# Sharing out the blocks of two accumulators in the first of five sweeps over a graph's matrix

## What is computed

```
# layer 0
h = tanh(concat([x, t]) @ W1 + b1);  XB = x @ B.T
x = layernorm(x + h @ W2 + b2 + adj @ XB - rowsum(adj) * XB)
# layer 1 (Chebyshev terms, K = 3): three more products with adj
T1 = adj @ x;  T2 = 2 * (adj @ T1) - x;  T3 = 2 * (adj @ T2) - T1
x = layernorm(x + x @ w[0] + T1 @ w[1] + T2 @ w[2] + T3 @ w[3] + bias)
# layer 2
h_neigh = (adj @ x + x) / max(rowsum(adj) + 1, 1)
x = layernorm(x + l2norm(relu(concat([x, h_neigh]) @ W + b)))
# layer 3: the last 100 non-zeros of each row, weighted by powers of 1/2
out = w(adj) @ (x @ weight) + bias;  x = layernorm(x + out)
```

## Time and profile before

| | |
|---|---|
| median of 3 runs | 3067.41 us (3066.72 to 3070.59) |
| the profiled execution | 3066.3 us |
| its span, first to last instruction | 3064.5 us |
| busy share, PE / DVE / ACT | 96% / 92% / 77% |
| DMA | 1148.18 MB, mean 375 GB/s, 9 tenths busy in nearly every slice |
| granted TensorE clock | 9 tenths or more in all 40 slices |
| chain that ended last | PE 67%, DVE 23%, DMA 4%, ACT 3% |

### The profile page before, as it was taken

One profiled execution on the slowest core, in us unless ns is written; L12 is line 12 of the kernel. 1 busy time (PEld: TensorE's weight loads), 2 busy tenths in 40 slices (PEclk: granted clock), 3 DMA queues, 4 the chain that ended last, 5 costly groups with the idle time before them and its releaser, 6 DMA issues.

```text
span 3064.5 us, 35311 instructions
## 1 busy us (share of the span) xinstructions
PE 2933.3 (96%) x13488; PEld 2156.4 (70%) x13488; DVE 2816.1 (92%) x2385; ACT 2356.8 (77%) x1631; POOL 13.2 (0%) x31
## 2 busy tenths in 40 slices
PE   7999999999999998999989999998989999999998
PEld 5677778777788886888867888776766555555554
DVE  7998988898998889988899988999999899999997
ACT  5887877777877678777777776877777788888887
POOL 0000000000000000000000000000000000000000
PEclk9999999999999999999999999999999999999999
DMA  9999999999999999999999999989999999999996
GB/s 345 391 389 353 385 358 355 363 391 375 366 397 382 377 377 391 391 384 378 378 374 370 381 377 376 374 344 350 402 404 409 359 387 384 380 387 384 380 384 252
DMA packets 158935, 1148.18 MB, mean 375 GB/s; under 512 B 18016, under 2 KB 18256, under 8 KB 19504
## 3 DMA queue, kind: packets, MB, share of 16 engines
q1 hardware_dynamic: 157312, 1143.02, 95.1%
q0 software_dynamic: 1088, 2.48, 0.2%
q10 hardware_dynamic: 368, 0.43, 0.0%
HBM read 1143.75 MB, written 2.10 MB: 374 GB/s over the span
## 4 chain that ended last, share of the span: by engine, by line
PE 67%; DVE 23%; DMA 4%; ACT 3%; issue 2%; SPq 0%; ACTq 0%; DVEq 0%
PE ACC L934 26%; DVE lo L660 18%; PE ACC L941 15%; PE ACC L1063 14%; DMA raw<-in_at 4%; PE PSF L1077 4%; PE PST L1077 4%; ACT hi L466 2%; PE PST L957 1%; DVE SV L770 1%; PE PSF L1043 1%; PE PSF L1018 1%; PE PSF L1021 0%; DVE SV L777 0%; PE PSF L1016 0%
## 5 line engine op out<-in xcount | busy, mean ns | idle before, releaser
L660 DVE TENSOR_TENSOR lo<-raw,hi 128x2048 fp32r<-128x2048 f32 x832 | 1877.9, 2287 | 151.6 <-ACT hi L466 146.7
L466 ACT CAST hi<-raw 128x2048 fp32r<-128x2048 f32 x832 | 1584.0, 1912 | 519.9 <-PE ACC L934 323.7
L934 PE MATMUL ACC<-hi,T 128*128 128x512 f32 x4992 | 1281.4, 393 | 6.1 <-DVE T L618 4.3
L934 PEld LDWEIGHTS ACC<-hi,T 128*128 128x128 f32 x4992 | 935.7, 189 | 208.1 <-DVE T L618 4.6
L941 PE MATMUL ACC<-lo,T 128*128 128x512 f32 x3200 | 888.7, 400 | 95.1 <-DVE lo L660 87.8
L941 PEld LDWEIGHTS ACC<-lo,T 128*128 128x128 f32 x3200 | 589.3, 189 | 294.1 <-DVE lo L660 179.5
L675 DVE SCALAR_TENSOR_TENSOR M<-raw,M 128x512 bf16<-128x512 f32 x1008 | 636.6, 686 | 41.3 <-PE ACC L1063 24.7
L472 ACT ACTIVATE Wf<-ACC,w_bias 128x1024 fp32r<-128x1024 f32 x512 | 568.1, 1114 | 128.6 <-PE ACC L1063 128.0
L1063 PE MATMUL ACC<-M,rank_b 128*128 128x512 bf16 x2032 | 528.4, 382 | 8.2 <-ACT Wf L472 6.7
L1063 PEld LDWEIGHTS ACC<-M,rank_b 128*128 128x128 bf16 x2032 | 158.8, 98 | 266.5 <-issue 131.6
L1077 PE MATMUL PST<-Wf,S 128*128 128x512 f32 x512 | 209.2, 489 | 0.0
(11 more groups left out here) (165 smaller groups left out, 983.2 us busy)
## 6 DMA issues: line engine op xcount, KB each, us to landing
raw<-in_at SPq DMA_DIRECT2D x1088, 1024.0 KB, 6.7
SV<-in_x_cols SPq DMA_DIRECT2D x8, 256.0 KB, 12.3
out<-O POOLq DMA_DIRECT2D x7, 256.0 KB, 6.6
out<-O ACTq DMA_DIRECT2D x1, 256.0 KB, 2.0
w_sb<-in_w POOLq DMA_DIRECT2D x3, 64.0 KB, 9.1
bias<-in_bias_rows ACTq DMA_DIRECT2D x1, 128.0 KB, 9.4
l1w_sb<-in_l_w POOLq DMA_DIRECT2D x2, 64.0 KB, 8.2
rank_f<-in_rank_mats POOLq DMA_DIRECT2D x1, 128.0 KB, 9.9
```

What stands on the lines that cost most here:

```text
L466: nc.scalar.copy(hi[:, c % NH], raw[:, c % NR]).then_inc(hi_done, 1)
L660: tt(lo[:, c % NR], raw[:, c % NR], hi[:, c % NH].bitcast(f32), ALU.subtract).then_inc(lo_done, 1)
L934: ins = mm(acc[:, part], w, hi[:, p.c % NH, s, part], start=p.opens and s == 0 and i == 0, stop=False)
```

## The change

The order of groups in sweep 1 is replaced from row 3 on by a written list of single blocks (four pairs each). A P block stands for the next block of that row's P group, an S block likewise. P and S blocks of a row now take turns, and S blocks of a row stand among P blocks of the next one. Both accumulators are then open at the same time. Rows 0 to 2, sweeps 2 to 5 and the last layer keep their order.

```diff
     if k == 1:
-        for r in range(NB):
-            single, older = ("S", r, blocks[r:]), ("P", r, blocks[:r])
-            out += [single] if r == 0 else [single, older] if r < 3 else [older, single]
+        for r in range(3):
+            out += [("S", r, blocks[r:])] + ([("P", r, blocks[:r])] if r else [])
+
+        order = ("P3 P3 S3 P3 S3 S3 P4 S3 S3 P4 P4 S4 P4 S4 P5 S4 P5 S4 P5 P5 S5 P5 S5 P6 P6 S5 "
+                 "P6 P6 P6 P6 S6 P7 P7 P7 S6 P7 P7 P7 P7 S7")
+        left = {f"P{r}": blocks[:r] for r in range(3, NB)} | {f"S{r}": blocks[r:] for r in range(3, NB)}
+        for name in order.split():
+            out.append((name[0], int(name[1:]), left[name][:1]))
+            left[name] = left[name][1:]
+        assert not any(left.values())
         return out
...
         for kind, r, blocks in sweep_groups(k, NB):
-            acc_of[k, kind, r] = turn % 2
-            turn += 1
+            whole = [J for other, row, piece in sweep_groups(k, NB) if (other, row) == (kind, r) for J in piece]
+            if (k, kind, r) not in acc_of:
+                acc_of[k, kind, r] = turn % 2
+                turn += 1
+                group_order.append((k, kind, r))
             for J in blocks:
                 for pr in range(NP):
                     pairs.append(Pair(len(pairs), k, r, kind, block_of(k, r, NB), J, pr,
-                                      J == blocks[0] and pr == 0, J == blocks[-1] and pr == NP - 1, pr == 0))
-            group_order.append((k, kind, r))
+                                      J == whole[0] and pr == 0, J == whole[-1] and pr == NP - 1, pr == 0))
             group_end[k, kind, r] = row_end[k, r] = pairs[-1].c
```

## The result

| | before | changed |
|---|---|---|
| median (6 runs each) | 3069.41 us | 3057.48 us |
| ratio, with 95% interval | | 0.9958 (0.9948 to 0.9968) |
| profiled execution | 3066.3 | 3057.9 |
| start to the end of row 2 | 288.2 | 286.6 |
| rows 3 to 7 of sweep 1 (from here on: the stretch) | 456.8 | 447.0 |

The prediction was 3054.4 us with a range of 3045 to 3066. As a ratio it was 3054.4 / 3067.4 = 0.9958; the two medians of six runs alone give 0.9961. The four parts of a profiled execution are cut at TensorE's signal after pairs 95, 255 and 831.

The account below looks back on a forecast made before the run. TensorE bounds double runs; in single runs it waits for VectorE, then the DMA queue, losing 25.0 us. Of this 7.9 + 0.6 + 2.0 + 1.5 = 12.0 stay, 13.0 are won: median 3054.4 us, range 3045 to 3066.

Parts of the forecast that it names:

- What bounds it: Rows 3 to 7: TensorE bounds double runs, but waits for VectorE, then the queue, in single runs; 25.0 us lost.
- (a): Single blocks right behind a P group's end (places 4, 13, 22, 30, 39), with ScalarE's copies: 7.9 us stay lost.
- (b): Single blocks alone between double blocks, without copies (places 2, 11, 15, 17, 20, 25, 34): 0.6 us stay lost.
- The rival in which each block pays 1.6 us: All fifteen single blocks: 23.7 of 25.0 us stay lost, 3066.1 us, no change; chance 0.21.
- (c): Single blocks that still touch (places 4 and 5; 7 and 8): 0.7 and 1.3, together 2.0 us stay lost.
- (d): Landings, places 4 to 8 and 11 to 17: TensorE asks faster than the queue's 2.48 us a pair; 1.5 us lost.
- the prediction's own sign that (d) is wrong: ScalarE idle ahead of its `hi` split until the landing, in many pairs of places 4 to 17; no size given.
- The sum: Rows 3 to 7: 12.0 of 25.0 us stay lost, 13.0 are won; profiled execution 3053.3 us, median 3054.4.
- No value and no accumulator waited for: P blocks needing a row's value start 12 pairs after its end, and groups open late enough: no new TensorE wait.
- rule of totals: Skill page: interleaving regimes with different most-contended engines may help; so read, the whole 25.0 us won, 3042.4 us.
- the rule on repeated bubbles: Skill page: a repeated gap can mean too few buffers; the three `hi` buffers stay three, so 0 won.

Follow-up runs that it names:

- small splits and transfers: Kernel before, the 60 single pairs of rows 3 to 7 transfer, split and subtract half their columns, all matmuls kept: stretch 436.3 us against 456.8.
- split copies: Changed kernel, ScalarE's second copy of a finished P group one pair later, from row 3 on: stretch 442.0 us, median 3055.39 us, ratio to before 0.9949.
- half transfers: Changed kernel, the 60 single pairs of rows 3 to 7 transfer half their data, `hi` and `lo` at full size: stretch 442.2 us against 447.0.

## Why the prediction was right, point by point

- **What bounds it.** Right. TensorE's own work was 431 us in all kernels (432 predicted), the loss was 25.9 (25.0 predicted), and with small splits and transfers it goes from the single runs.
- **(a) The five blocks behind a P group.** Predicted 2.3, 1.3, 2.0, 1.3 and 1.0, together 7.9; measured 1.3, 1.3, 1.9, 1.3 and 1.3, 7.1; the 2.3 for place 4 was 1.0 too high. That the pile of `tanh` and copies moves to row 5 was right (1.9 at place 22, 1.3 at place 13), and the split copies showed the cause.
- **(b) Blocks alone.** Right for six of the seven: places 2, 11, 15, 20, 25 and 34 cost 0.34 us together (0.6 predicted). The rival in which each block pays 1.6 us fell with them. The seventh, place 17, was to last 7.2 to 7.4 us and lasted 9.4; that belongs to the next point.
- **(c) and (d), touching blocks and landings.** These terms were mis-sized: 2.0 + 1.5 = 3.5 predicted, and places 5, 7, 8 and 17 cost 7.9, or 6.7 in the second profile of the same kernel. The step that failed stands in both. (c) let VectorE's 2.22 us set the pace of places 7 and 8, with 2.0 us given back in place 6; (d) said "The six slots of `raw` lend some two or three pairs, and the double blocks ahead fill them". The trace has landings 2.48 us apart from pair 118 (place 5) to pair 139 (place 10), but for the late one, and ScalarE's split starts within 0.1 us of its landing in every pair of places 7, 8 and 17, and in 24 of the 56 pairs of places 4 to 17. That was the prediction's own sign that (d) is wrong. At this pace a double block gives back 4 x (2.72 - 2.48) = 1.0 us and a single one uses up 2.7, so place 6 had not filled the slots again. With half transfers the four places cost 1.7: some 5 of the 6.7 us are landings' (places 18 and 26 rose by 1.7 there, so the stretch fell by less). The bound of 5.9 us for (d) was for places 11 to 17 alone, and its 2.27 us a pair should be 2.20, as four single and three double blocks stand there; most of what the landings cost fell in places 5 and 8.
- **The sum.** 9.8 us were won in the stretch (11.5 in the second profile) and not 13.0. The rest of the medians' 11.9 isn't the change's in any way that I could show: the profiled execution is 8.4 faster, from 1.6 at the start, 9.8, 0.6 in sweeps 2 to 5, and 3.6 lost in the last layer (below). The start, the same code in every kernel, took 286 to 292 us in the twelve profiles, so parts outside the stretch scatter by more than the 3.2 us that the sum was off. That the recorded ratio is 0.9958 to the last digit is luck; that the time is in the range isn't, as the stretch alone puts it there.
- **No value and no accumulator waited for**, as predicted: the double blocks that open a group or need a new value cost 0.4 us or less.
- **The two readings of the Trainium skill's page.** The Trainium skill's "Perfetto Trace Analysis" (section "Optimization Strategy") read as a rule of totals promised the whole 25.0; the run gave 9.8 of it. Read as the rule on repeated bubbles it promised nothing, and 9.8 us of such waits went with no buffer added. Neither gave the size: what did was how many pairs of lead a double block gives back.

## What to carry to other kernels

Where two kinds of work on one stream are bound by different engines, take turns in pieces that the lead of the buffers can cover, and work out the lead that each piece uses up and gives back, for every stage of the stream: here VectorE's balance was positive at four pairs each (2.0 us given back, 1.6 used up), the queue's was not (1.0 and 2.7). This rule is worked out from the paces; no run changed the number of buffers or the length of the pieces. Once such turns have made the common engine the bound, small piles on other engines (two copies in a row) begin to cost what a long wait hid before: parting them won 2.2 to 3.8 us in the new order and nothing in the old one, counted to one pair past the stretch. Count past the end of the stretch, too: 1.2 us of what seemed won there had moved to the next pair. And when the stretch that was changed wins less than execution times scatter, compare its length in the profiles and not only the medians.

## What the runs showed of the hardware that I had not expected

**After nearly the same pause of TensorE the clock fell in one kernel and not in the other.** The last layer has the same instructions in every kernel, yet it took 728.9 us in both profiles of the changed kernel, 725.3 in the one before (725.2 to 725.7 in seven others), and 726.9 and 727.0 in two. Windows of the changed kernel (first TensorE's busy time, the clock is the third number from the end):

```profile
2352.80:2356.20 3.40, 1.40 (x7) 0.77 (x8) 3.30 (x7) 3.19 (x4) 0.00 (x0) 1.00 1.01 422
2356.20:2359.60 3.40, 3.40 (x10) 1.42 (x10) 3.33 (x7) 1.89 (x2) 0.00 (x0) 0.50 1.01 422
...
2369.70:2373.20 3.50, 1.40 (x7) 0.70 (x6) 2.90 (x7) 3.29 (x4) 0.00 (x0) 1.00 0.98 405
...
2980.80:2984.20 3.40, 1.30 (x6) 0.58 (x4) 2.16 (x4) 3.36 (x5) 0.00 (x0) 1.00 1.01 381
2984.20:2987.60 3.40, 3.36 (x8) 1.42 (x9) 1.46 (x3) 2.02 (x2) 0.00 (x0) 0.50 0.87 361
```

The first and the last of these places in the kernel before, 12.0 us later as its sweep 5 ends 12.0 us later:

```profile
2364.80:2368.20 3.40, 1.44 (x7) 0.81 (x8) 3.30 (x7) 3.19 (x4) 0.00 (x0) 1.00 1.01 419
2368.20:2371.60 3.40, 3.40 (x18) 1.75 (x16) 3.33 (x7) 2.93 (x3) 0.00 (x0) 1.00 1.01 422
...
2992.80:2996.20 3.40, 1.55 (x7) 0.82 (x8) 1.12 (x3) 3.19 (x4) 0.00 (x0) 1.00 1.01 390
2996.20:2999.60 3.40, 3.40 (x17) 1.83 (x16) 3.37 (x7) 2.85 (x3) 0.58 (x1) 1.00 0.58 207
```

At 0.50 of full speed, so at 1.2 GHz, TensorE did 10 and 8 matmuls where it did 18 and 17 at 2.4 GHz: some 1.7 us lost at each, and 3.6 in the whole layer. All of these falls stand right behind a pause of TensorE. Both kernels have one at a further place (at 2373 in the changed one, after the middle row, and at 2383 in the one before); at the other two places TensorE was busy for 1.40 and 1.30 us of the 3.4 ahead in the changed kernel and the clock fell, and for 1.44 and 1.55 in the one before and it did not. The two kernels with 726.9 and 727.0 us have two such falls, those near 725.3 have one. Why the same place falls in one kernel and not in another, no run here settles.

**A landing can be 2.1 us late in a full queue.** At 372 us one 16 KB packet of the instruction queue ran among those of pair 129's transfer, which landed 4.6 us after the one ahead of it where 2.5 is the rule. Such packets come every 1.5 to 38 us in this stretch of both traces. Whether one of them causes such a delay was not tried, but the twelve traces can be counted. They have 1253 full-sized pairs of the stretch that were issued over 2.8 us before the one ahead had landed. With such a packet in the 2.4 us after that landing, 46 of 168 landed over 3.1 us behind it; without one, 93 of 1085. So the packets go with late landings, but most late landings have none.
